# fp16 halves of the normalised rows, turned by a transposing DMA instead of TensorE

## What is computed

```python
x = x + tanh(g_xattn) * expert_layer(layernorm(x), token_ids, W)   # W = Wg = Wu = Wd = ctx_2048 (4,512,512)
x = x + tanh(g_ffn)   * low_rank_moe(layernorm(x), Wr, br, Wd, bd, Wu, bu)
# expert_layer: e = token_id // (25000 // 4);  g = silu(h @ W[e].T);  u = h @ W[e].T;  y = (g * u) @ W[e].T
# low_rank_moe: 8 experts of rank 16, softmax router, the best two, weights normalised to 1
```

## Time and profile before

| | |
|---|---|
| median of 3 runs | 200.31 us (199.83 to 200.53) |
| the profiled execution | 200.81 us, of it 198.7 us span from first to last instruction |
| PE busy | 173.7 us (87%), 1074 matmuls and transpositions |
| DVE busy | 155.5 us (78%) |
| ACT busy | 105.9 us (53%) |
| POOL busy | 99.5 us (50%) |
| mean granted clock of TensorE | 0.986 of full speed |

### The profile page before, as it was taken

The page is one execution under the profiler, slowest core; times in us unless marked ns, Lnnn a source line. Parts: engine busy times, 40 slices in busy tenths (PEclk is TensorE's granted clock), DMA queues, the critical chain, the costliest instruction groups (busy, mean ns, idle before and its releaser), DMA issues.

```text
span 198.7 us, 4382 instructions
## 1 busy us (share of the span) xinstructions
PE 173.7 (87%) x1074; PEld 105.5 (53%) x1075; DVE 155.5 (78%) x523; ACT 105.9 (53%) x224; POOL 99.5 (50%) x246
## 2 busy tenths in 40 slices
PE   1666896999998999999999999999999999987550
PEld 1654473665554555756567565665655666553310
DVE  4859695797669799898988899877887778877840
ACT  3596599984576365363635646256462653415300
POOL 4477855508444475465735538336062351626551
PEclk9999999999999999999999999999999999999995
DMA  4937682000301201103011010110110101001121
GB/s 144 383 136 243 209 214 80 30 26 2 107 4 49 56 0 53 58 2 106 3 53 54 0 53 0 53 54 0 53 53 2 53 2 53 35 21 53 53 101 57
DMA packets 6784, 13.43 MB, mean 68 GB/s; under 512 B 2392, under 2 KB 2520, under 8 KB 6768
## 3 DMA queue, kind: packets, MB, share of 16 engines
q0 software_dynamic: 2560, 8.39, 12.6%
q1 hardware_dynamic: 4208, 4.86, 7.3%
HBM read 9.06 MB, written 4.19 MB: 67 GB/s over the span
## 4 chain that ended last, share of the span: by engine, by line
PE 66%; issue 7%; DMA 7%; DVE 7%; POOL 7%; SPq 1%; ACT 1%; POOLq 1%; DVEq 1%
PE ps_y L603 8%; PE ps_y L605 8%; PE ps_y L604 8%; PE ps_a L603 7%; PE ps_a L604 7%; PE ps_a L605 7%; PE ps_pT L624 4%; DMA xs<-in_x_dram,rows_of 4%; PE ps_h2T L685 3%; PE ps_hT L677 3%; DMA bu_nat<-in_L_ffn_bu_dram 3%; POOL hot_slot L432 2%; POOL xs L439 2%; PE ps_hid L632 2%; PE ps_hid L634 1%
## 5 line engine op out<-in xcount | busy, mean ns | idle before, releaser
L456 POOL TENSOR_SCALAR ve<-mv 128x1 f32<-128x1 f32 x32 | 7.6, 238 | 60.6 <-DVE mv L1099 50.1
L603 PE MATMUL ps_y<-w_hi,pT_hi 128*128 x76 | 28.8, 379 | 2.6 <-DVE w_lo L952 1.8
L783 ACT ACTIVATE pT_hi<-ps_pT 128x512 f16<-128x512 f32 x19 | 11.3, 595 | 36.0 <-PE ps_pT L624 36.0
L603 PE MATMUL ps_a<-w_hi,hT_hi 128*128 x76 | 29.6, 389 | 0.7 <-DVE hT_lo L1074 0.6
L604 PE MATMUL ps_a<-w_lo,hT_hi 128*128 x76 | 29.5, 388 | 0.0
L605 PE MATMUL ps_a<-w_hi,hT_lo 128*128 x76 | 29.3, 386 | 0.0
L604 PE MATMUL ps_y<-w_lo,pT_hi 128*128 x76 | 28.8, 379 | 0.0
L605 PE MATMUL ps_y<-w_hi,pT_lo 128*128 x76 | 28.8, 379 | 0.0
L796 ACT ACTIVATE h<-xs,mrs,rs 128x512 f32<-128x512 f32 (+1 forms) x16 | 13.0, 814 | 21.6 <-POOL mrs L458 21.6
L1086 DVE SCALAR_TENSOR_TENSOR xs<-ps_y,y_t,xs 128x512 f32 x19 | 14.3, 751 | 12.2 <-PE ps_y L605 11.5
L457 POOL TENSOR_TENSOR rs<-ve,neg_half 128x1 f32<-128x1 f32 x32 | 18.8, 587 | 2.7
(11 more groups left out here) (209 smaller groups left out, 432.6 us busy)
## 6 DMA issues: line engine op xcount, KB each, us to landing
w_nat<-in_ctx_dram SPq DMA_DIRECT2D x4, 1024.0 KB, 7.5
xs<-in_x_dram,rows_of POOLq DMA_INDIRECT x16, 3.5
wd_nat<-in_L_ffn_Wd_dram SPq DMA_DIRECT2D x1, 256.0 KB
wu_nat<-in_L_ffn_Wu_dram SPq DMA_DIRECT2D x1, 256.0 KB
out_dram<-xs,rows_of POOLq DMA_INDIRECT x16, 2.9
b_in<-in_L_ffn_bd_dram SPq DMA_DIRECT2D x1, 64.0 KB
bu_nat<-in_L_ffn_bu_dram SPq DMA_DIRECT2D x3, 16.0 KB
tok_i<-in_itok_BxS_dram SPq DMA_DIRECT2D x1, 8.0 KB, 1.6
```

Source lines behind the costliest of these rows:

```text
L603: mm(ps[:, :], lhs_hi[:, kc, :], hi, start=(kc == 0), stop=False)
```

## The change

The pairs 0 and 1 stay as they are. For pairs 2 to 18 ACT, behind `h`, also writes the high half `hh[:, 0]` (a copy to fp16 out of SBUF, in the row layout); POOL subtracts it from `h` and writes the low half `hh[:, 1]` (`h_low`, at the head of POOL's iteration k-1); SP turns both halves with one transposing DMA of 128 x 1024 fp16 into `hT` (`turn`), which now has two buffers, taken in turns. PE waits for this DMA (`hT_in`) before the product. PE's four transpositions, ACT's `hT_hi` and DVE's `hT_lo` are gone for these pairs. `h` and `hh` have one buffer each, so ACT waits for POOL (`hh_lo_done`) before it writes the next `h`, and for the DMA (`hT_in`) before it writes the next high half. SP issues the turn of pair k ahead of passing on the arrival of the tile after k + 4.

```diff
-        hT_hi = sb("hT_hi", [P, KC, P], fp16)
-        hT_lo = sb("hT_lo", [P, KC, P], fp16)
+        hh = sb("hh", [P, 2, D], fp16)
+        hT = sb("hT", [P, 2, 2, KC, P], fp16)
...
+        FLIP = 2
...
+            def turn(k):
+
+                sp.wait_ge(hh_lo_done, k + 1 - FLIP)
+                sp.wait_ge(a_done, k - 1)
+                sp.dma_start_transpose(hT[:, k % 2, :, :, :].rearrange("p s c q -> p (s c) q"),
+                                       hh[:, :, :].rearrange("p s d -> p (s d)")).then_inc(hT_in, 16)
...
             for t in range(T):
                 sp.wait_ge(s_gather[t], 16)
                 sp.sem_inc(x_in, 1)
+                if t >= 4 + FLIP:
+                    turn(t - 4)
...
+            for k in range(T - 4, NP):
+                turn(k)
...
+            def h_low(k):
+
+                pool.wait_ge(hh_hi_done, k + 1 - FLIP)
+                g.tensor_tensor(hh[:, 1, :], h[:, :], hh[:, 0, :], ALU.subtract).then_inc(hh_lo_done, 1)
+
...
             for i in range(-3, T + LATE + 5):
+                if FLIP <= i + 1 < NP:
+                    h_low(i + 1)
                 k = i - 3 - LATE
...
-                    pe.wait_ge(hT_lo_done, k + 1)
-                    split_product(ps_a, hT_hi, hT_lo, e_now).then_inc(a_done, 1)
+                    if i0 < FLIP:
+                        pe.wait_ge(hT_lo_done, k + 1)
+                    else:
+                        pe.wait_ge(hT_in, (k + 1 - FLIP) * 16)
+                    split_product(ps_a, hT[:, buf, 0, :, :], hT[:, buf, 1, :, :], e_now).then_inc(a_done, 1)
...
-                if some(NP, 1, i0):
+                if some(NP, 1, i0) and i0 + 1 < FLIP:
                     k = i + 1
                     pe.wait_ge(normed1, k + 1)
                     for c in range(KC):
...
-                if some(NP, 1, i0):
+                if some(NP, 1, i0) and i0 + 1 < FLIP:
                     k = i + 1
                     act.wait_ge(hT_done, k + 1)
-                    wait_last(act, a_done, k)
-                    a(hT_hi[:, :, :], ps_hT[:, :, :], ACT.Copy).then_inc(hT_hi_done, 1)
+                    a(hT[:, k, 0, :, :], ps_hT[:, :, :], ACT.Copy).then_inc(hT_hi_done, 1)
...
                     act.wait_ge(rstd1, k + 1 if some(T, 2, i0) else T)
-                    wait_last(act, hT_done, k)
+                    if i0 + 2 <= FLIP:
+                        wait_last(act, hT_done, k)
+                    else:
+                        act.wait_ge(hh_lo_done, k - FLIP)
                     a(h[:, :], flat(xs[:, col(tile), :]), ACT.Identity,
                       bias=mrs[:, 0, col(tile)], scale=rs[:, 0, col(tile)]).then_inc(normed1, 1)
+                    if i0 + 2 >= FLIP:
+                        act.wait_ge(normed1, k + 1)
+                        if i0 + 2 > FLIP:
+                            act.wait_ge(hT_in, (k - FLIP) * 16)
+                        a(hh[:, 0, :], h[:, :], ACT.Copy).then_inc(hh_hi_done, 1)
...
-                if some(NP, 1, i0):
+                if some(NP, 1, i0) and i0 + 1 < FLIP:
                     hT_low(i + 1)
```

More of the change, by code:

```diff
@@ L272, in bass_flamingo_gated_kernel @@
         hT_lo_done = sem("hT_lo_done")
+        hh_hi_done = sem("hh_hi_done")
+        hh_lo_done = sem("hh_lo_done")
+        hT_in = sem("hT_in")
         a_done = sem("a_done")
@@ L331, in pipeline @@
                     with eng.Fori(0, (last - first) // 2) as n:
-                        step(n * 2 + (first + odd), first)
-                        step(n * 2 + (first + odd + 1), first)
+                        step(n * 2 + (first + odd), first, buf=(first + odd) % 2)
+                        step(n * 2 + (first + odd + 1), first, buf=(first + odd + 1) % 2)
                 first = last
@@ L650, in experts_of, with step @@
                         expert_of(i) if some(NP, 0, i0) else None)
-            def step(i, i0, experts=None, meanwhile=None):
+            def step(i, i0, experts=None, meanwhile=None, buf=None):
+                buf = i0 % 2 if buf is None else buf
                 has_y, has_a = some(NP, -1, i0), some(NP, 0, i0)
@@ L774, in ffn_high_parts, with step @@
                 a(bu3[:, :], bu_nat[:, :], ACT.Copy, scale=s_ffn[0:Q3, 1:2]).then_inc(s_ffn_hi, 1)
-            def step(i, i0, meanwhile=None):
+            def step(i, i0, meanwhile=None, buf=None):
                 if some(NP, -1, i0):
@@ L1073, in hT_low @@
                 dve.wait_ge(hT_hi_done, k + 1)
-                v.tensor_tensor(hT_lo[:, :, :], ps_hT[:, :, :], hT_hi[:, :, :],
+                v.tensor_tensor(hT[:, k, 1, :, :], ps_hT[:, :, :], hT[:, k, 0, :, :],
                                 ALU.subtract).then_inc(hT_lo_done, 1)
```

## The result

The changed kernel takes 204.63 us (median of 4 runs, 203.65 to 205.90) against 200.07 us of the kernel before on the same chip: ratio 1.024, 95% interval 1.016 to 1.032, 2.4% slower. The profiled execution took 205.9 us with a span of 204.0 us, 5.3 us more than the span of 198.7 before. In later groups of runs the kernel before had 201.1 to 201.2 us, so all further kernels are compared by their ratio. Ratios leave disturbed runs out; where too few were left for an interval, the kept runs are named.

A forecast was written before the change was run, and what follows sets the result against it. PE was taken to set the pace in steps 7 to 17, 8.33 us each. Early +3.6 and middle +2.2 gave +5.8 us on the profiled 200.81, so 206.6; the median, 0.5 lower, 206.1 us; range 201 to 215.

The forecast's parts named there:

- Two of its signs: Middle steps: PE's busy share below 95%, and the transposition of the product every 8.4 to 8.7 us.
- Removal worth at most 0.44 us a step, and not got: PE, steps 7 to 17: four transpositions gone give at most 0.44 us a step; PE waits for DVE and POOL instead.
- The subtraction in the round: POOL, between reciprocal root and choice: 1.16 us more, 0.60 less on DVE, minus slack used; +0.2 us a step, 11 steps.
- 0.23 of it is DVE's own: DVE's 0.61 us wait before adding y: reading in which 0.23 us is not usable slack, making a step +0.18 us.
- 0.05 us shorter: Middle round of DVE and POOL: reading in which all 0.61 us of slack goes, a step 0.05 us shorter.
- +0.18: Middle round of DVE and POOL: us added per step if 0.23 of the 0.61 us wait is DVE's own.
- L: Transposing DMA on SP, 256 KB: latency from the subtraction's end to landing, taken as 3.5 us, ends 1.6 and 7.5.
- The estimate of 10.5 us: Transposing DMA: eight 128x128 blocks at 1.309 us each by the skill's VectorE page, which spoke against the change.
- the second rival: Single-buffer hh ring: the DMA sets the pace from L = 6.4 on; 231 us at 7.5 us; chance 0.08.
- The early steps: Up to pair 4: ACT's wait for hh costs 2.3 us, then PE waits for the DMA; +3.6 us in all.
- Rival 1: Middle and early steps: faster, subtraction hidden (perhaps in POOL's pause) and DMA quick; about 197 us, chance 0.11.

The follow-up runs named there:

- x_idle: Changed kernel with POOL's subtraction for pairs 6 to 18 moved to the end of the iteration before, in POOL's pause: 198.67 us, ratio 0.983.
- x_from6_idle: Changed kernel with the DMA only from pair 6 on and POOL's subtraction in its pause for all these pairs: 196.04 us, ratio 0.976.
- b_head: Kernel before plus one unread POOL subtraction per step between reciprocal root and choice, from step 6 on, no DMA: 207.33 us, ratio 1.034.
- x_from6: Changed kernel with the DMA turning h only from pair 6 on, earlier pairs over TensorE: 202.01 us, ratio 1.005.
- x_behind: Changed kernel with POOL's subtraction behind the choice of the two experts, no longer ahead of it: 204.9 us, ratio 1.022.
- x_two: Changed kernel with two buffers of hh, the DMA's semaphore one for each: median 203.97 us; runs kept 201.94 and 202.68 us.
- x_warm: Changed kernel with the four transpositions of pair 2 left on PE, their result unread: 204.4 us, ratio 1.017.
- x_all: Changed kernel with subtraction behind the choice, two buffers of hh and pair 2's four transpositions left on PE: 203.04 us, ratio 1.010.

## Why the prediction was right, and which of its steps were not

The time (206.1 us forecast, 204.63 measured) and the sign were right, for the profiled execution 206.6 against 205.9. That the size fits so well is in part luck: the prediction took 2.2 us too much in the middle steps (0.0 came) and 1.4 us too little in the early ones (3.6 against 5.0), and the two errors nearly cancel. Two of its signs failed narrowly: PE was busy for 95.8% of the middle steps, not below 95%, and a step took 8.35 us, not 8.4 to 8.7. Point by point:

- **Removal worth at most 0.44 us a step, and not got.** Right. x_idle and x_from6_idle get 0.40 of it, 7.95 us a step; the changed kernel stays at 8.35.
- **The subtraction in the round.** The mechanism was right (b_head: +6.9 us by the subtraction alone), its size too large: +0.2 us a step was taken, +0.00 came in the changed kernel's profile, +0.07 in that of x_from6 (92.56 us for eleven steps, before 91.79). The step that failed is "0.23 of it is DVE's own": y is added at 138.16 directly behind the low-rank sum, so none of that wait was DVE's. The round without a wait measures 8.18 us (second statistics end at 131.68 and at 139.86; POOL's next operations begin 0.09 us later), the next one, with the wait for y, 8.74, and the mean of ten is 8.35. The 7.60 us of b_head give the same: 7.60 + 1.16 - 0.60 = 8.16. A second slip is in the comparison: the prediction set its sums beside the one round of 8.48 and not beside the step of 8.33, so that "0.05 us shorter" with all slack used is 8.43, 0.10 longer than a step, and its +0.18 is +0.33.
- **L.** 3.5 us was taken from the gather; from the end of the subtraction (54.81) to PE's start (58.05) 3.2 us were measured, 3.08 of them on the chain as the DMA. The Trainium skill, "Advanced Engine Details and Errata" (X-Bar Transpose (TRN2)), which holds a transposing DMA to be as fast as a plain one, fits: 256 KB turned take about as long as the 3.5 us of the gather. The estimate of 10.5 us, worked out from one block's time in the Trainium skill, "VectorE: DVE Perf Modes" (The three transpose paths), does not hold here. Nor does the second rival: in the middle steps PE never waits for the DMA.
- **The early steps.** Right in their places: the high halves of pairs 3 and 5 wait 1.80 and 2.15 us on ACT, and PE waits 1.62 us for the DMA at pair 4. The sum was 3.6 us; 5.0 us came in the profiled execution, and by the ratios of the changed kernel and x_from6 1.9%, 3.8 us. The prediction took ACT's wait as the only delay up to pair 2, 2.3 us. In the profile it was 4.0 us on another path: 1.05 us by the held-up `b_in`, 0.35 by the later load, and 12 matmuls at 0.43 instead of 0.22 us, 2.5 us. What the prediction missed is that POOL's subtraction holds up operations of DVE; it counted POOL's queue only. Its own path can be read alone in x_behind, whose early part is the same program: there `b_in` fell ahead of the subtraction (0.17 us), the clock stayed at 1.00, and ACT's wait for pair 3 was 2.06 us. Pair 2 then started at 40.91, 0.84 us late, and pair 4 at 55.10, 2.1 us late: ACT's wait reached PE by less than the 2.3 us taken, and the rest of the early loss hangs on what the small load, `b_in` and the clock do in an execution.
- **Rival 1** named the way out and its price: the subtraction in POOL's pause, 11 x 0.44 = 4.8 us less. x_from6_idle gives 4.9, at 196.04 us. (By its own terms the rival's "about 197" is 200.3 - 4.8 + 0.8 = 196.3.) It was rightly not the forecast, since the order put the subtraction elsewhere.

Two things stay open. Why the clock fell in some executions and not in others could not be settled: after a PE pause of 3.82 us in the changed kernel, not after 3.81 us in x_idle; with the transpositions left on PE it fell too. And what PE's 0.6 to 1.0 us ahead of `ps_hid` is in every second step: `h2T_lo` had ended at 137.59 and PE's last matmul at 137.71, yet the next began at 138.60, and the profile names no releaser. Between 80 and 163 us it was there five times in each of the changed kernel, x_behind, x_two, x_warm and x_all (3.0 to 3.5 us in all), and gone in x_idle, so it comes with the subtraction in the round. That it is the turn of PE's loop, which takes two steps at a time, is only a guess.

## What to carry to other kernels

Work that is moved off the bound engine must be placed where the receiving engine idles in every round, not only where it has time on average: POOL was half idle, and the same 1.16 us a step cost 6.9 us in all between the root and the choice (b_head) and nothing that can be seen in its pause. Before a large POOL operation is put beside DVE work, look which DVE operations due at that time read two tensors in SBUF, like `w`, or are of the kind of `b_in`, a TENSOR_SCALAR of a few columns in SBUF: those were held up here. And a single buffer with a DMA of 3 us in its ring can make an engine wait: ACT stood 1.80 and 2.15 us for it in the early steps, though what that alone costs is not settled (x_two), and in the middle it cost nothing (x_idle).

## What the runs showed of the hardware

While POOL's 128x512 subtraction runs, some operations of DVE do not get on. `w`, which reads two tensors in SBUF, took 972 ns on average in x_behind instead of 247 ns; `gap`, the difference of two columns in SBUF, 0.93 us instead of 0.17; `b_in`, a TENSOR_SCALAR in SBUF, 1.22, 1.68 and 1.86 us instead of 0.17; each ended within 0.05 us of POOL's end where the rows are shown. Others run on: operations that read PSUM (`add_y` 0.75 us inside the subtraction), and the statistics, which read one tensor in SBUF, 0.69 us inside and outside. Two such rows of the changed kernel, and POOL's beside them:

```profile
75.17 0.93 DVE L1179 TENSOR_TENSOR gap<-top 128x1 f32<-128x1 f32 x1
...
100.00 0.69 DVE L1093 BATCH_NORM_STATS2 st<-xs 128x6 f32 x1
```
```profile
74.92 1.15 POOL L521 TENSOR_TENSOR hh<-h,hh 128x512 f16<-128x512 f32 x1
...
99.37 1.16 POOL L521 TENSOR_TENSOR hh<-h,hh 128x512 f16<-128x512 f32 x1
```

The Trainium skill says in "SBUF — State Buffer" (Who interferes with whom) that a DVE instruction with two SBUF inputs contends with a GpSimd instruction that reads SBUF, that tensor_scalar can contend through its two-port modes, and that in those whoever issues first gets the shared ports for the whole instruction and the other is fully blocked. The trace agrees for `w` and `gap`. For `b_in` no run shows the mode, and its row begins ahead of the subtraction's, by 0.02 us in the changed kernel, 0.48 in x_idle and 0.66 in x_warm, and yet it is the one that is held up:

```profile
32.04 1.86 DVE L1038 TENSOR_SCALAR b_in<-b_in 128x8 f32<-128x8 f32 x1 [1.97 <-DMA bu_nat<-in_L_ffn_bu_dram]
```
```profile
31.58 1.09 POOL L455 DMA_INDIRECT xs<-in_x_dram,rows_of  x1 [0.16 <-issue]
32.70 1.16 POOL L521 TENSOR_TENSOR hh<-h,hh 128x512 f16<-128x512 f32 x1
```

POOL issues a gather at that moment. Beside such a gather `b_in` took 0.17 us in the kernel before, with no subtraction behind it, and in x_behind, where it began 0.93 us ahead of the subtraction. What holds it from its start on is open.

The 17 transposing DMAs brought no such hindrance: with 69 GB/s in the middle instead of 36, x_idle's PE was busy without a break.
